# A Householder step with W read from PSUM, alpha y.u as a column, and the row product on the live columns

## The reference

```python
def _L0_gnn_ref(features, A, W1, b1, W2, b2):
    ...
    L_norm = d_inv_sqrt[:, None] * L * d_inv_sqrt[None, :]
    _, U = jnp.linalg.eigh(L_norm)
    agg = jnp.einsum('mn,bnd->bmd', U.T, features)
    h = jax.nn.relu(agg @ W1 + b1)
    out = h @ W2 + b2
    return jnp.einsum('nm,bmd->bnd', U, out)
...
h = jnp.maximum(_layernorm(x, axis=-1), 0.0)
x = x + _L0_gnn_ref(h, adj, L0_gnn_W1, L0_gnn_b1, L0_gnn_W2, L0_gnn_b2)
h = jnp.maximum(_layernorm(x, axis=-1), 0.0)
x = x + _L1_gnn_ref(h, adj, L1_gnn_Wg0, ...)
```

## Time and profile before

| | |
|---|---|
| three runs | 1312.48, 1313.9, 1313.9 us (median 1313.9) |
| profiled execution | 1313.11 us, span of the core 1311.1 us |
| busy over the span | PE 1227.2 us (94%), DVE 944.3 (72%), ACT 918.2 (70%), POOL 341.3 (26%) |
| 56 to 304 us, Householder | PE 244.94 of 248 us, DVE 237.13, ACT 203.99, POOL 207.29, granted clock 1.00 |
| 304 to 460 us | DVE 150.22 of 156 us, PE 94.42, ACT 95.22, POOL 117.88, granted clock 0.84 |
| 460 to 1311 us | PE 836.39 of 851 us, ACT 583.48, DVE 508.60, granted clock 1.00 |

### The profile page before, as it was taken

The page is one execution under the profiler, slowest core; times in us unless marked ns, Lnnn a source line. Parts: engine busy times, 40 slices in busy tenths (PEclk is TensorE's granted clock), DMA queues, the critical chain, the costliest instruction groups (busy, mean ns, idle before and its releaser), DMA issues.

```text
span 1311.1 us, 26414 instructions
## 1 busy us (share of the span) xinstructions
PE 1227.2 (94%) x7961; PEld 1075.2 (82%) x7961; DVE 944.3 (72%) x4624; ACT 918.2 (70%) x3309; POOL 341.3 (26%) x1206
## 2 busy tenths in 40 slices
PE   9999999998663699999999999999999999999997
PEld 7777777786553588789889989889889899899897
DVE  8999999999999957757755655645645645655655
ACT  5777788886995122478578579579578578578576
POOL 0388888888888300000300000000000000000000
PEclk9999999998797899999999999999999999999999
DMA  9500000000000023100100100100100100000001
GB/s 264 140 1 1 2 2 2 2 2 1 1 1 1 1 64 97 33 1 1 33 0 0 32 0 0 32 0 0 32 0 0 32 0 13 19 0 16 17 1 33
DMA packets 43631, 28.86 MB, mean 22 GB/s; under 512 B 1520, under 2 KB 39440, under 8 KB 43536
## 3 DMA queue, kind: packets, MB, share of 16 engines
q1 hardware_dynamic: 43536, 27.81, 7.7%
HBM read 19.42 MB, written 8.39 MB: 21 GB/s over the span
## 4 chain that ended last, share of the span: by engine, by line
PE 72%; DVE 21%; ACT 4%; issue 1%; DMA 1%; ACTq 0%; DVEq 0%; SPq 0%
PE bank L941 15%; PE bank L931 11%; PE bank L936 9%; PE bank L944 8%; PE bank L717 3%; PE bank L733 3%; PE bank L861 2%; PE bank L737 2%; PE bank L913 2%; PE bank L905 2%; PE bank L869 2%; PE bank L726 2%; PE bank L728 2%; PE bank L876 2%; PE bank L884 2%; PE bank L899 2%
## 5 line engine op out<-in xcount | busy, mean ns | idle before, releaser
L654 ACT ACTIVATE BIG<-bank,bias 128x128 f32<-128x128 f32 (+2 forms) x544 | 226.7, 417 | 161.6 <-PE bank L944 102.1
L941 PE MATMUL bank<-spare,wT 128*128 128x256 f32 (+2 forms) x1408 | 311.3, 321 | 0.0
L654 ACT ACTIVATE PV<-bank,bias 128x256 f32<-128x256 f32 (+2 forms) x704 | 301.6, 431 | 0.0
L941 PEld LDWEIGHTS bank<-spare,wT 128*128 128x128 f32 x1408 | 234.8, 191 | 13.2
L931 PE MATMUL bank<-spare,wT 128*128 128x128 f32 (+2 forms) x1088 | 226.4, 319 | 4.1 <-DVE spare L1662 2.7
L1648 DVE TENSOR_TENSOR BIG<-BIG,PV 128x128 f32<-128x128 f32 (+2 forms) x192 | 63.0, 328 | 207.6 <-ACT BIG L654 207.5
L931 PEld LDWEIGHTS bank<-spare,wT 128*128 128x128 f32 x1088 | 169.5, 191 | 19.2 <-DVE spare L1662 6.1
L944 PE MATMUL bank<-spare,wT 128*128 128x128 f32 (+2 forms) x768 | 169.7, 303 | 0.0
L936 PE MATMUL bank<-spare,wT 128*128 128x128 f32 (+2 forms) x768 | 141.7, 307 | 3.7 <-DVE spare L1660 1.2
L662 ACT ACTIVATE spare<-spare 128x256 f32<-128x256 f32 (+2 forms) x352 | 133.0, 378 | 4.2 <-DVE spare L1651 3.9
L944 PEld LDWEIGHTS bank<-spare,wT 128*128 128x128 f32 x768 | 125.2, 191 | 3.3
(11 more groups left out here) (495 smaller groups left out, 2752.0 us busy)
## 6 DMA issues: line engine op xcount, KB each, us to landing
spare<-in_x SPq DMA_DIRECT2D x32, 256.0 KB, 3.7
out<-X SPq DMA_DIRECT2D x32, 256.0 KB, 2.4
spare<-in_L_gnn_Wih SPq DMA_DIRECT2D x4, 256.0 KB, 4.8
spare<-in_L_gnn_Whh SPq DMA_DIRECT2D x4, 256.0 KB, 4.4
W<-in_L_gnn_W SPq DMA_DIRECT2D x2, 64.0 KB, 3.0
Wg<-in_L_gnn_Wg SPq DMA_DIRECT2D x2, 64.0 KB, 2.6
adj<-in_adj SPq DMA_DIRECT2D x1, 64.0 KB, 1.8
X<-in_x SPq DMA_DIRECT2D x4, 0.5 KB, 17.4
```

What stands on the lines that cost most here:

```text
L654: last = nc.scalar.activation(gate_out[q][i][:, 0:T], gate(i, q, T), ACT.Tanh if q == GATE_G else ACT.Sigmoid, bias=bias[:, at:at + 1])
L941: last = nc.tensor.matmul(gate(i, q, T), wT[:, 0, p - 1, q * D:(q + 1) * D], xt, start=True, stop=(j == 0))
```

## The change

In the reflector HXA is gone. The sum's result is multiplied by alpha into a column of its own, ACU, and the next column of U is HX ACU + YA in place of HXA y.u + YA. W is made in the reflector, straight from bank 4 (ACOL + AM times the bank), in front of the next column, so that `update` no longer has it between Z and the first update of A. Z is a plain sum of bank 1 and ACU. The row product is taken on the live columns alone. The filler has t // 2 columns more, step 16 gets six filler products of 128 columns in front of its P, and ACT makes the row of eta ahead of both statistics. The sum waits for AM too.

```diff
@@ act
-                statistic(2 * k)
                 if t + 1 < N:
                     act.wait_ge(xb_ready, 2 * k + 2)
                     act.wait_ge(hv, at_hv(k, ETA))
                     nc.scalar.activation(eta_row[:, t + 1:N], banks[3][:, t + 1:N], ACT.Copy,
                                          scale=eta[:, t:t + 1]).then_inc(taken, 1)
+                statistic(2 * k)
                 statistic(2 * k + 1)
@@ pe
-                nc.tensor.matmul(banks[2][:, 0:N], x_wide, A[:], start=True, stop=True).then_inc(yrow_ready, 1)
+                nc.tensor.matmul(banks[2][:, from_t], x_wide, A[:, from_t], start=True, stop=True).then_inc(yrow_ready, 1)
                 if t + 1 < N:
                     nc.tensor.matmul(banks[4][:, 0:1], A[:], x_c, start=True, stop=True).then_inc(ycol_ready, 1)
+                    if k == LEAF:
+                        keep_clock(6, B[5])
                     pe.wait_ge(taken, taken_by(k, COL_U))
                     nc.tensor.matmul(banks[1][:, 0:N], S_(UC).to_broadcast([N, N]), A[:],
                                      start=True, stop=True).then_inc(p_ready, 1)
-                idle(IDLE_BEHIND)
+                idle(IDLE_BEHIND + t // 2)
@@ dve, reflector
                     n_hx = step(V.tensor_tensor(S(HX), S(XA), eta[:, t:t + 1], ALU.mult))
+                    dve.wait_ge(hv, n_am)
                     dve.wait_ge(taken, taken_by(k, ROW))
...
-                dve.wait_ge(hv, n_hx)
-                step(V.tensor_tensor(S(HXA), S(HX), alpha[:, t:t + 1], ALU.mult))
                 dve.wait_ge(ycol_ready, k + 1)
                 n_ya = step(V.scalar_tensor_tensor(out=S(YA), in0=banks[4][:, 0:1], scalar=S(AM), in1=nudge[:, t + 1:t + 2],
                                                    op0=ALU.mult, op1=ALU.add))
-                return n_uy, n_ya
+                dve.wait_ge(hv, n_uy)
+                n_acu = step(V.tensor_tensor(S(ACU), uyB[:, t:t + 1], alpha[:, t:t + 1], ALU.mult))
+                dve.wait_ge(taken, taken_by(k, COLUMN))
+                step(V.scalar_tensor_tensor(out=S(W_), in0=banks[4][:, 0:1], scalar=S(AM), in1=S(ACOL),
+                                            op0=ALU.mult, op1=ALU.add))
+                return n_acu
@@ dve, update
-                V.scalar_tensor_tensor(out=column(t), in0=S(HXA), scalar=uyB[:, t:t + 1], in1=S(YA),
+                V.scalar_tensor_tensor(out=column(t), in0=S(HX), scalar=S(ACU), in1=S(YA),
                                        op0=ALU.mult, op1=ALU.add).then_inc(x_ready, 1)
                 dve.wait_ge(p_ready, k + 1)
-                n_z = step(V.scalar_tensor_tensor(out=S(Z_), in0=alpha[:, t:t + 1], scalar=uyB[:, t:t + 1],
-                                                  in1=banks[1][:, t:t + 1], op0=ALU.mult, op1=ALU.add))
-                dve.wait_ge(taken, taken_by(k, COLUMN))
-                n_w = step(V.tensor_tensor(S(W_), S(YA), S(ACOL), ALU.add))
+                n_z = step(V.tensor_tensor(S(Z_), banks[1][:, t:t + 1], S(ACU), ALU.add))
                 step(V.scalar_tensor_tensor(out=A[:, live(k)], in0=banks[1][:, live(k)], scalar=S(HX),
                                             in1=A[:, live(k)], op0=ALU.mult, op1=ALU.add))
-                dve.wait_ge(hv, n_w)
+                dve.wait_ge(hv, n_z)
```

More of the change, by code:

```diff
@@ L189, in build @@
         STEPS = N - 1
-        XM, XA, HX, YA, HXA, W_, Z_, V_, ACOL, UC, AM = range(10, 21)
+        XM, XA, HX, YA, ACU, W_, Z_, V_, ACOL, UC, AM = range(10, 21)
         def sigma(k):
@@ L1061, in reflector @@
                 if last:
-                    return n_uy, None
-                dve.wait_ge(hv, n_hx)
-                step(V.tensor_tensor(S(HXA), S(HX), alpha[:, t:t + 1], ALU.mult))
+                    return n_uy
                 dve.wait_ge(ycol_ready, k + 1)
@@ L1073, in below_of, with update @@
                 return step(V.tensor_tensor(S(XM), column(k), minus_below[:, k + 1:k + 2], ALU.mult))
-            def update(k, n_uy, n_ya):
+            def update(k, n_acu):
                 t = k + 1
-                dve.wait_ge(hv, n_ya)
-                V.scalar_tensor_tensor(out=column(t), in0=S(HXA), scalar=uyB[:, t:t + 1], in1=S(YA),
+                dve.wait_ge(hv, n_acu)
+                V.scalar_tensor_tensor(out=column(t), in0=S(HX), scalar=S(ACU), in1=S(YA),
                                        op0=ALU.mult, op1=ALU.add).then_inc(x_ready, 1)
                 dve.wait_ge(p_ready, k + 1)
-                n_z = step(V.scalar_tensor_tensor(out=S(Z_), in0=alpha[:, t:t + 1], scalar=uyB[:, t:t + 1],
-                                                  in1=banks[1][:, t:t + 1], op0=ALU.mult, op1=ALU.add))
-                dve.wait_ge(taken, taken_by(k, COLUMN))
-                n_w = step(V.tensor_tensor(S(W_), S(YA), S(ACOL), ALU.add))
+                n_z = step(V.tensor_tensor(S(Z_), banks[1][:, t:t + 1], S(ACU), ALU.add))
                 step(V.scalar_tensor_tensor(out=A[:, live(k)], in0=banks[1][:, live(k)], scalar=S(HX),
                                             in1=A[:, live(k)], op0=ALU.mult, op1=ALU.add))
-                dve.wait_ge(hv, n_w)
+                dve.wait_ge(hv, n_z)
                 n_v = step(V.scalar_tensor_tensor(out=S(V_), in0=S(HX), scalar=S(Z_), in1=S(W_),
@@ L1106, in _ @@
             for k in range(LEAF):
-                update(k, *reflector(k))
+                update(k, reflector(k))
             dve.wait_ge(taken, 1)
@@ L1116, in _ @@
             for k in range(LEAF, STEPS):
-                n_uy, n_ya = reflector(k)
+                n_acu = reflector(k)
                 if k + 1 < STEPS:
-                    update(k, n_uy, n_ya)
+                    update(k, n_acu)
             def go(ins):
```

## The result

The changed kernel takes 1300.8 us (median of four runs, 1300.5 to 1301.5); the kernel before took 1313.9 in the same comparison. The ratio is 0.9903 with a 95% interval from 0.9886 to 0.9920, so 13.1 us less. The prediction was 1302.8 with a range from 1298.5 to 1307.5. The profiled execution has a span of 1298.8 us, where it was 1311.1.

A forecast was written before the change was run, and what follows sets the result against it. The Householder loop through DVE and PE bounded the first 304 us; steps (15 us) and leaf (1.0) ended it about 16 sooner, GpSimd cut that to 11.5, a slow clock to 11.1: 1313.9 to 1302.8, range 1298.5 to 1307.5.

The forecast's parts named there:

- the sum has 15: Householder steps: 38 gain 0.147 us each, 17 gain 0.165 and 72 gain 0.10, 15 us in all.
- The column part: Householder step, DVE: first update of A starts 0.13 us earlier behind the column; zero gained between sum and column.
- The third wait: Ahead of the sum: shares one waiting instruction with two old waits; zero, upper bound 0.07 us a step.
- floor (c): Late Householder steps: the square root holds the sum's start at 0.96 plus 0.70 = 1.66 us behind the column.
- The live columns: Row product: 0.83 ns saved per dropped column, only the last pass counting, where PE still ties the sum.
- Statistics: ScalarE: both statistics behind the row of eta, the same instructions in another order; zero.
- The leaf: After step 15: six filler products fill PE's 1.41 us gap and keep the clock; 1.0 us, bounds 0 and 1.2.
- Rival 4: Late steps: fewer live columns let PE's clock fall, each cold step 1.0 us longer; 1335 with 32 cold; chance 0.04.
- 432.1 at the soonest: GpSimd's leaf end; slowed beside the refinements by 1.28 it ends at 436.0, leaving 11.5 us gain at L1540.
- Rival 2: Leaf beside the refinements: GpSimd hardly suffers, the gain is 15 to 16 us, 1298.4; chance 0.12.
- The prediction's first rival: Refinements: GpSimd is blocked and moves only while the DVE is free; gain 1 to 2 us, 1312.4; chance 0.03.
- (3): Householder steps: third wait or W's slot sits in the chain; gain only 5 to 8 us, 1307; chance 0.13.

The follow-up runs named there:

- the full row product: The changed kernel with the row product taken on all 128 columns again; 1302.94 us, ratio 0.9920.
- HX in one instruction: The changed kernel with HX = (XM alpha) eta in one scalar-tensor-tensor instead of two tensor-tensors; 1296.72 us, ratio 0.9868.

## Why the prediction was right, and where it was not

**The total** was 1302.8 against 1300.8 and in the range, from two errors that partly cancel: the stage gave 12.2 us and not 16, and GpSimd, which was to take 4.5 of them back, took none. That the median came so near is luck. The ordinary steps alone gave 10.9 where the sum has 15 (its last term, 72 steps by 0.10, is 7.2 and not 7.0, which makes it 15.6).

**The column part.** Right where PE ties the sum. The first update of A at 0.20, nothing gained or lost between sum and column, and the loop shorter by 0.14 at t = 38; the forecast there was 0.16 and a period of 2.21, measured 2.23.

**The third wait** was taken at zero, with an upper bound of 0.07 a step. It costs 0.03 ahead of the sum and 0.05 behind it. The prediction has it share one waiting instruction with the two old ones: it does, and that instruction then takes 0.050 us instead of 0.021. Ahead of the sum it lifts the DVE's floor behind the sign product from 0.70 to 0.74, so that the late sum stays at 1.69 instead of the 1.66 of floor (c). In 126 steps that is some 4 us (0.03 times 126 is 3.8), about the size of what is missing from the 15. I saw the 0.74 in the earlier trace rows and took it for PE's; before, it was, since the kernel without the third wait and with live columns comes to 0.71.

**The live columns** have the right price, 0.83 ns each, up to the floor: 2.1 us of the total, seen in the full row product and, without the other part, at t = 63 and t = 99. (The 0.11 us for 128 columns that it rests on are 0.86 ns.) The reason given, that only the last pass counts, is not what the trace has: the second pass starts 0.213 us behind the first with 128 columns and 0.180 with 90, so that the first pass shortens too.

**Statistics** zero: right.

**The leaf.** Its mechanism was right, and its size where the clock comes back (1.0 us) too. Its upper bound of 1.2 was badly wrong. I bounded it by the one step at 1.2 GHz that the earlier trace rows shows, and took for granted that the clock comes back as it did there. In the changed kernel without the filler it does not, and the filler's worth is 142 us in five executions of six. Rival 4 had the mechanism, fewer columns and a falling clock, but put it at the late steps; it lies at the gaps of the leaf and of the first steps. At the leaf the filler products of the same change keep it away.

**GpSimd** is the step that failed. "432.1 at the soonest" held the slowing of GpSimd fixed to its sweeps. Behind the stage the sweeps take 23 to 34 us where they take 22.5 beside it, depending on which instructions of the two engines meet. At the end of the stage GpSimd was 19.7 us into its eleventh sweep before and is 10.4 us into it now, which leaves 9.2 us more, yet it took only 4.9 us more (from 302.5 to 434.3, and from 290.3 to 427.0). The last piece took 10.5 us where it was 15.1 in the earlier trace rows; beside the refinements 8.9 (HX in one instruction), so the factor there is 1.05 to 1.07 and the forecast's 1.28 was too high. Rival 2 had that part right. Its 1298.4 is what my steps would have given without GpSimd, 2.4 us too low.

The factor of 1.76 in the earlier trace rows belongs to the DVE instructions that this piece happened to meet, not to a busy DVE as such. In the kernel before it met wide ones, here with the three multiplications of L393:

```profile
421.81 0.68 DVE L1444 TENSOR_SCALAR RC<-RC 128x1024 f32<-128x1024 f32 x1
421.92 1.88 POOL L393 TENSOR_TENSOR leaf<-leaf 1x15 f32<-1x15 f32 x3
...
422.53 1.19 DVE L1449 SCALAR_TENSOR_TENSOR BIG<-EV,sc,RC 128x508 f32<-128x508 f32 x1
```

With HX in one instruction the same three stand beside DVE instructions of 128 columns:

```profile
423.00 0.57 POOL L393 TENSOR_TENSOR leaf<-leaf 1x15 f32<-1x15 f32 x3
```

The last of the three takes 1.09 us in the kernel before, from 422.71 on, and ends 0.08 behind L1449; beside the Householder steps it takes 0.21. In the changed kernel the piece starts behind these wide instructions, beside ones of at most 0.43 us, and takes 10.5.

The Trainium skill, page "SBUF — State Buffer", section "SBUF: two separate sides", has one of the two engines hold the shared ports for its whole instruction while the other blocks fully; of DVE instructions outside the two-port modes it says so only of those with two SBUF inputs, and only against a GpSimd instruction that reads SBUF. Instruction by instruction the rows agree: L1449 reads two SBUF tensors (EV and RC), and L393 ends with it. For a whole stretch it gives no factor: beside a DVE busy for 7.74 of 8.90 us with short instructions GpSimd lost 0.4. The prediction's first rival took it so, and fell. Why the short ones cost so little was not tested.

**The rivals.** (1) fell with GpSimd's 9 us to spare. (3) has the right mechanism, the third wait in the chain, and half its price. The forecast was carried by errors of opposite sign.

## What to carry to other kernels

Where a stage repeats a step a hundred times, a semaphore wait on the critical engine has a price of its own even if what it waits for is long done; measure it in an ordinary step before taking zero. When the granted clock is 1.00 only because PE is kept busy, an edit that takes PE work away must be tried alone and several times: one execution can look fine. And of an engine that runs beside the main chain, ask how much it has to spare by delaying it, not by adding up how slow it may become: a slowing read from one place holds for the instructions that met there.

## What the runs showed of the hardware that I had not expected

With the same program and a gap of 1.41 us in front of one product, the time shows no long cold stretch in one execution of six (1301.45 us), and in the others the kernel took 1443 to 1444 us; in the profiled one of these the granted clock stayed at 0.50 for 399 us, with PE's records filling all windows of the stage. Putting t of 128 columns back into one product brought five executions of five through the same gap. A third wait in front of an instruction costs 0.03 us where two were there already, because the sequencer's waiting instruction takes 0.050 us instead of 0.021. GpSimd's sweep of equal instructions takes between 22.0 and 34.0 us beside the DVE, and a single multiplication of 15 elements 0.21 or 1.09 us.
